# Attention maxima split into two parts behind their transposition, and two batches' gathers moved into a feed-forward part

## The reference, cut to what matters

```python
anchor_B = qk @ W_anchor.T * SCALE            # logits: 64 anchors for each row and head
attn = jax.nn.softmax(anchor_B, axis=-1)
s = jnp.sum(attn, axis=-2)
out = jnp.einsum('bhna,bhnd->bhad', attn, v)
out = recip[..., None] * out                  # recip: 1 / s
out = jnp.einsum('bhna,bhad->bhnd', attn, out)
...
h = jax.nn.silu(_tlin(x, w1_w, w1_s)) * _tlin(x, w2_w, w2_s)
h = jax.nn.gelu(_tlin(h, h1_w, h1_s), approximate=False)
h = jax.nn.gelu(_tlin(h, h2_w, h2_s), approximate=False)
return _tlin(h, w3_w, w3_s)
```

## Time and profile before

| | us |
|---|---|
| median of 3 runs (804.94 to 808.8) | 805.0 |
| profiled execution, its time | 807.5 |
| its span | 805.8 |
| PE busy in the span | 658.6 |
| DVE, ACT, POOL busy | 567.5, 401.3, 270.6 |

### The profile page before, as it was taken

One profiled execution on the slowest core, in us unless ns is written; L12 is line 12 of the kernel. 1 busy time (PEld: TensorE's weight loads), 2 busy tenths in 40 slices (PEclk: granted clock), 3 DMA queues, 4 the chain that ended last, 5 costly groups with the idle time before them and its releaser, 6 DMA issues.

```text
span 805.8 us, 9652 instructions
## 1 busy us (share of the span) xinstructions
PE 658.6 (82%) x2985; PEld 474.4 (59%) x2985; DVE 567.5 (70%) x1443; ACT 401.3 (50%) x699; POOL 270.6 (34%) x228
## 2 busy tenths in 40 slices
PE   5855444029999997788989999989899989899897
PEld 2755444028888886344557754567656468555575
DVE  5876386317898883799587678877686976784663
ACT  4552313317777773244257544367444385442573
POOL 6652717700000004779312067302177202242100
PEclk9985755559999997599899999999999999999999
DMA  6404248477889851000000010000000000000000
GB/s 204 131 31 152 77 166 303 167 262 256 269 261 330 285 179 59 26 13 27 14 0 1 1 46 21 13 2 1 29 24 27 0 1 1 26 1 1 0 1 27
DMA packets 26211, 69.26 MB, mean 86 GB/s; under 512 B 5344, under 2 KB 8432, under 8 KB 24688
## 3 DMA queue, kind: packets, MB, share of 16 engines
q1 hardware_dynamic: 22064, 60.24, 21.9%
q0 software_dynamic: 4096, 8.40, 3.4%
HBM read 46.46 MB, written 22.16 MB: 85 GB/s over the span
## 4 chain that ended last, share of the span: by engine, by line
PE 56%; DVE 18%; issue 7%; POOL 6%; ACT 5%; another core or an unknown queue 3%; DMA 3%; SPq 1%; DVEq 0%; ACTq 0%; POOLq 0%
PE ps L1702 14%; PE ps L1698 8%; PE ps L1704 8%; PE ps L1706 6%; PE ps L1705 6%; PE ps L1959 6%; POOL yb L653 2%; DVE stats L1065 2%; PE ps L1977 2%; PE ps L1947 2%; DVE ring L1584 2%; POOL misc L701 1%; DVE cmat L1658 1%; DVE yb L1484 1%
## 5 line engine op out<-in xcount | busy, mean ns | idle before, releaser
L653 POOL DMA_INDIRECT yb<-y_by_expert,ypos x64 | 64.8, 1013 | 166.6 <-DMA y_by_expert<-ysb 151.0
L1702 PE MATMUL ps<-hid,fh 128*128 128x512 f32 x256 | 103.6, 405 | 5.3 <-DVE hid L1568 5.3
L1704 PE MATMUL ps<-hid,fh 128*128 128x512 f32 x256 | 101.4, 396 | 0.0
L607 POOL DMA_INDIRECT rows_by_expert<-h,pos x64 | 64.7, 1011 | 53.4 <-DVE pos L1226 34.8
L701 POOL TENSOR_TENSOR misc<-misc,ring 128x1024 f32<-128x1024 f32 x28 | 66.1, 2360 | 32.6 <-DVE ring L1558 27.5
L1568 DVE TENSOR_TENSOR hid<-ring,hid 128x512 fp32r<-128x512 f32 x56 | 38.6, 689 | 42.0 <-ACT hid L944 40.1
L1959 PE MATMUL ps<-ring,hn 128*128 128x512 f32 x112 | 57.1, 634 | 9.2 <-DVE ring L1558 9.2
L1702 PEld LDWEIGHTS ps<-hid,fh 128*128 128x128 f32 x256 | 48.2, 188 | 21.3 <-DVE hid L1568 10.6
L1977 PE MATMUL ps<-attnT,cmat 128*128 128x512 f32 x128 | 56.9, 592 | 0.0
L1704 PEld LDWEIGHTS ps<-hid,fh 128*128 128x128 f32 x256 | 48.3, 189 | 10.7
L1002 ACT ACTIVATE ring<-ps 128x1024 f32<-128x1024 f32 x32 | 32.8, 1024 | 43.4 <-PE ps L1947 41.6
(11 more groups left out here) (324 smaller groups left out, 1702.9 us busy)
## 6 DMA issues: line engine op xcount, KB each, us to landing
wbuf<-w_split SPq DMA_DIRECT2D x46, 512.0 KB, 5.6
w_split<-parts SPq DMA_DIRECT2D x4, 2048.0 KB
raw<-in_w SPq DMA_DIRECT2D x8, 512.0 KB
xs<-rows_by_expert SPq DMA_DIRECT2D x16, 256.0 KB, 5.5
y_by_expert<-ysb SPq DMA_DIRECT2D x16, 256.0 KB, 4.7
rows_by_expert<-zeros SPq DMA_DIRECT2D x9, 256.0 KB, 2.2
xa<-in_x SPq DMA_DIRECT2D x4, 512.0 KB, 4.8
ffn_raw<-in_ffn SPq DMA_DIRECT2D x2, 1024.0 KB
```

The costliest lines, as they stand in the source:

```text
L607: gp.indirect_dma_start(disp, bass.IndirectOffsetOnAxis(pos[:, b, k, t:t + 1].bitcast(U32), 0), h1[:, b % 2, t, :], None).then_inc(scatter ...
L653: gp.indirect_dma_start(yb[:, k, t, :], None, ydisp, bass.IndirectOffsetOnAxis(ypos[:, b, k, t:t + 1].bitcast(U32), 0))\
L1702: te.matmul(out_, w(0), x(0), start=first, stop=False)
L1704: return te.matmul(out_, w(0), x(1), start=False, stop=last_)
```

## The change

Two things are changed. First, DVE no longer splits the maxima ahead of the transposition. The 128x16 maxima are transposed whole; ACT's copy to `mTs`, rows 0 to 15, is the rounded part, and DVE takes the remainder from PSUM, 16x128, into rows 32 to 47 of `mTs` (`max_remainder`, event `dve_mlo`). Rows 16 to 31 are zero, set once. `shift`, and the half-1 transposition that overwrites bank 1, wait for `dve_mlo` in the place of `act_maxT`. `max_remainder(t)` stands in DVE's queue behind `sums(t-1)`, and for tile 0 behind the second `neg_max` (batch 0) or the residual of the feed-forward part (the other batches). Second, POOL's gathers for batches 2 and 3 are taken out of the attentions of batches 1 and 2 and stand behind the modulation in the feed-forward part of batches 0 and 1. Those for batch 1 stay.

```diff
-        onehot = sb("onehot", [32, 1024], F32R)
+        onehot = sb("onehot", [48, 1024], F32R)
...
-        mTs = sb("mTs", [32, 128], F32R)
+        mTs = sb("mTs", [48, 128], F32R)
...
-        m32 = sb("m32", [128, 2, 2 * H], F32R)
...
+        dve_mlo = Events(sem("dve_mlo"), ts)
...
-                if more:
-                    gather(b + 1, places[0:2])
+                if b == 0:
+                    gather(1, places[0:2])
...
-                    if more and t < T - 2:
-                        gather(b + 1, places[2 * t:2 * t + 2])
-                if more:
-                    gather(b + 1, places[2 * (T - 2):])
+                    if b == 0 and t < T - 2:
+                        gather(1, places[2 * t:2 * t + 2])
+                if b == 0:
+                    gather(1, places[2 * (T - 2):])
...
                     for g in gs2:
                         modulate(g, b + 1)
+                if b + 2 < B:
+
+                    gather(b + 2, places)
...
-                copy(mTs[:, :], ps[0:32, 1, 0:128]).then_inc(*act_maxT.raise_(t))
+                copy(mTs[0:H, :], ps[0:H, 1, 0:128]).then_inc(*act_maxT.raise_(t))
...
+            v.tensor_copy(mTs[:, :], zeros[0:48, 0, :])
...
             def neg_max(t, b):
                 dve.wait_ge(*pe_logits.now(t, b))
-                k0, i = 2 + 2 * (t % 2), t % 2
-                if t >= 2:
-                    dve.wait_ge(*dve_max.now(t - 2, b))
-                settle(b, v.tensor_reduce(nmax[:, i, :], ps[:, k0:k0 + 2, :].rearrange("p k (h a) -> p (k h) a", a=A),
-                                          X, ALU.max, negate=True))
+                k0 = 2 + 2 * (t % 2)
                 if t >= 2:
                     dve.wait_ge(*pe_maxT.now(t - 2, b))
-                settle(b, v.tensor_copy(m32[:, i, 0:H], nmax[:, i, :]))
-                v.tensor_tensor(m32[:, i, H:2 * H], nmax[:, i, :], f(m32[:, i, 0:H]), ALU.subtract)\
-                    .then_inc(*dve_max.raise_(t))
+                v.tensor_reduce(nmax[:, t % 2, :], ps[:, k0:k0 + 2, :].rearrange("p k (h a) -> p (k h) a", a=A),
+                                X, ALU.max, negate=True).then_inc(*dve_max.raise_(t))
+
+            def max_remainder(t, b):
+
+                dve.wait_ge(*act_maxT.now(t, b))
+                v.tensor_tensor(mTs[32:32 + H, :], ps[0:H, 1, 0:128], f(mTs[0:H, :]), ALU.subtract)\
+                    .then_inc(*dve_mlo.raise_(t))
...
                     sums(t - 1, b)
+                    if t < T:
+                        max_remainder(t, b)
                     scaled(t - 1, b)
...
                 residual("F", 0, ffn_bank(0, "y"), b)
+                if more:
+                    max_remainder(0, b + 1)
...
-                transposes(1, [f(m32[:, t % 2, :])], 32).then_inc(*pe_maxT.raise_(t))
+                transposes(1, [nmax[:, t % 2, :]], H).then_inc(*pe_maxT.raise_(t))
 
             def shift(t, b):
-                pe.wait_ge(*act_maxT.now(t, b))
+                pe.wait_ge(*dve_mlo.now(t, b))
...
                     if h == 1 and t + 2 < T:
-                        pe.wait_ge(*act_maxT.now(t + 2, b))
+                        pe.wait_ge(*dve_mlo.now(t + 2, b))
```

More of the change, by code:

```diff
@@ L235, in build @@
         a_raw = at("a_raw", 0, [128, H * A])
-        oh_f = at("oh_f", 48, [32, 1024])
+        oh_f = at("oh_f", 48, [48, 1024])
         tri_f = at("tri_f", 52, [128, 128])
@@ L589, in _ @@
                              pattern=[[1, 128]], channel_multiplier=-1).then_inc(u_pool, 1)
-            for base in (0, -H):
+            for base in (0, -32):
                 v = oh_f[:, :].rearrange("p (h a) -> p h a", h=H)
@@ L1616, in _ @@
             neg_max(1, 0)
+            max_remainder(0, 0)
             hT_attn(1, 0)
@@ L1620, in _ @@
                 sums(0, b)
+                max_remainder(1, b)
                 if b == 0:
@@ L1628, in _ @@
                 sums(1, b)
+                max_remainder(2, b)
                 scaled(1, b)
@@ L1633, in _ @@
                 sums(2, b)
+                max_remainder(3, b)
                 scaled(2, b)
```

## The result

The changed kernel took 830.3 us (median; 829.5 to 838.0) where the kernel before took 805.0: a ratio of 1.0333, 95% interval 1.026 to 1.041. I had forecast 816.0, range 807 to 822. The sign is right, the size is not: plus 25 where I had plus 11. The execution that was profiled is one of 838.0 us, so its trace holds some 8 us that the median does not. Ratios and intervals are made of each kernel's fast runs alone (a run over 1.5% above its kernel's fastest counts as slow) and medians of all runs, so a ratio can differ from the quotient of the medians beside it.

The account below looks back on a forecast made before the run. The prediction took PE to bound batches 1 to 3, and POOL and DVE to hold batch 0. Terms 7.65 + 2.7 + 0.6 = 10.95, say 11.0, on 805.0 gave 816.0 us, range 807 to 822.

Parts of the forecast that it names:

- the gathers' new place: Sixteen gathers behind the modulation in each of two feed-forward parts, forecast to hold DVE's CASTs: 0.6 us in all.
- So it fits: Claim that the moved gathers, 20 us or somewhat more, end at 464 to 465, before the first product at 465.79.
- The wait of half 1: In attention tiles, half 1 of PE's transpositions waits for DVE's remainder; period 5.16 to 5.66, plus 0.50 us a tile.
- tiles 3 to 5: Tiles t = 3, 4, 5 of batches 1 to 3: 0.50 us each, 1.50 a batch.
- the next: Tile t = 6 of batches 1 to 3: 0.50 less 0.10 for the removed CAST, 0.40 us.
- the last: Tile t = 7 of batches 1 to 3: no logits follow, product already waiting for DVE's scaling, forecast 0.
- At the start: Start of attentions 1 to 3: 0.34 us for t = 2, and 0.31 for the first shift behind tile 0's remainder.
- Batch 0: Attention held by POOL and DVE: first shift 1.04 us late, remainders of tiles 2 and 3 later; 2.7 us in all.
- What was taken out: Gathers removed from the attentions of batches 1 and 2, forecast to give 0 in the tiles and behind them.
- the part on the maxima: The forecast's terms for the new wait: 7.65 us for batches 1 to 3 and 2.7 for batch 0.
- gathers too late: Rival: all sixteen gathers held, ending at 475, 9 us past the product behind them, in two batches; 834 us, chance 0.05.

## Why the prediction was wrong

**The step that failed** is the gathers' new place, which I had at 0.6 us (0.3 for each of two batches, with bounds of 0 and 1.0). "So it fits" was right: they end at 469.3, ahead of the product L686 at 479.9, and DVE's CASTs were hardly held (0.43 to 0.60 us beside them). But I had asked only what the gathers wait for and whom they hold by the shared memory, not what a row of sixteen does to the events of everybody else. In the first comparison the two stretches that hold them grew by 13.6 us together; beside the whole change without a stall (83.92 and 79.83) they are 9.1 and 5.6 us longer. Gathers alone, on a like chip, grew them by 4.7 and 4.8 against the other chip's 79.5 and 79.7. The case that this needs both edits was excluded. Eight gathers did nothing and pauses removed the stall, on a chip where sixteen in a row were not run, and traffic of the DMA engines does not do it on a chip without the stall. The warning stood in the trace of before, in sixteen scatters of layer 0 and the row of DVE behind "remote".

**The wait of half 1** was right in kind and nearly in size. On the clock of the tile the forecast and the trace agree step by step from the product on: sum at 1.19 (measured 1.16), reciprocal at 2.44 (2.42), remainder at 2.61 (2.70), its end at 2.90 (2.98), half 1 at 3.01 (3.10), and from there 2.65 us to the next product (2.65). The 0.09 is the hand-over from reciprocal to remainder, 0.28 between their starts where I took 0.17 from a range up to 0.25. The remainder takes 0.28 (I had 0.29 between 0.17 and 0.44). That it is a wait and not more work is shown by the run with the logits between the halves, which brings the period to 4.96, under that of before.

**By tile**, from the exponentials of batch 3 (intervals before: 3.49, 6.30, 5.15, 5.15, 5.15, 5.26, 3.94; after: 3.69, 6.43, 5.75, 5.75, 5.75, 5.75, 4.35): tiles 3 to 5 cost 0.60 each (I had 0.50), the next 0.49 (0.40), the last 0.41, which I had at 0 because its product waited for DVE's scaling anyway. That last one is the larger error: in DVE's queue the scaling stands behind the remainder too, which I read in the code only afterwards. At the start 0.33 over two intervals and 0.05 ahead of them, where I had 0.34 and 0.31. A batch costs 3.0 instead of 2.55, three batches 9.0 instead of 7.65.

**The clock at the start of attention 1** was not in the sum. PE's short waits there are followed in some runs by about 7 us at the lower clock, and the attention takes 39.4 instead of 37.45: 1.9 us more (in three of five runs with the new maxima and the old order, beside the first).

**Batch 0**, 2.7 in the forecast, is confirmed by rows only in its first step:

```profile
336.12 1.22 DVE L1541 TENSOR_REDUCE nmax<-ps 128x16 f32<-128x1024 f32 x1 [0.94 <-PE ps L1719]
336.23 0.27 ACT L730 ACTIVATE mTs<-ps 16x128 fp32r<-16x128 f32 x1 [6.21 <-PE ps L1711]
...
337.71 0.73 PE L1960 MATMUL ps<-onehot,mTs 48*128 48x512 f32 x2 [1.52 <-DVE mTs L1547]
```

The first shift starts 1.48 us behind the start of ACT's copy, where it was 0.32 before (332.56 and 332.88): 1.16 late, forecast 1.04. The whole of the batch can't be read off. Its stretches differ between runs with the same code there: attention 0 and what follows take 129.5 us in the trace of before, 125.8 with the gathers alone, 129.3 in the kernel before with the copies beside it, and 129.4 with the maxima alone. What is left of the maxima alone, 13.3 - 9.0 - 1.9 = 2.4 us of medians, is near it. Two small slips in the prediction's own numbers move no sum: 345.6 - 343.19 is 2.4 and not 2.45, and 4 x 0.8 is 3.2 and not 3.3.

**What was taken out** gave nothing, as forecast: attention 2 has 37.45 us with gathers in it (maxima alone) and without.

So the part on the maxima, 10.35 us by forecast, is 13.3 on the second chip and 12.8 by its ratio on 805 (11.4 to 14.2 by the interval). The gathers alone, by their ratio where they stall, are 7.2 of 805 (3.1 to 11.3), where I had 0.6. The two make 20 of the 25 us; with the 1.0223 of the maxima alone at 797 they make 25. The rest is within the intervals and was not assigned. Where nothing stalls, the whole change gives 1.0181 and 1.0195, which is 820 to 821 on 805 and inside the forecast's range. That would have been partly luck, since there the gathers cost nothing and the maxima 2 to 3 us more than forecast.

The chance of 0.05 for "gathers too late" at 834 was near the time for a wrong reason: nothing waited for the gathers.

## What stays open

What it is in such a chip that delays the events was not found. In six rows of gathers (two feed-forward parts of three traces) the first late event was one that PE raised 11 to 13 gathers into the row, and it was recorded 1.8 to 4.7 us late, at the 13th gather or behind it. The Trainium skill says in "DMA: Bandwidth & Descriptors", section "Why a DMA increments its semaphore by 16 and not by 1", that all 16 DMA engines add to the semaphore for each such DMA. The traces at 774 us agree, with 16 recorded updates a gather (1024 for 64 in eight of the ten, 1021 and 1015 in the others); those at 797 to 807 have 8 to 12 a gather. That other engines' updates queue up with these would fit both the late events and the missing records, but no run here shows it, and it would have to differ between chips.

The profile records these updates, and whether the recording has a part in the stall, no run tells either. That instructions are fetched late does not fit the rows: the waiting engine starts 0.02 to 0.03 us behind the record of its event, and POOL goes on. The two runs with traffic were not made on a chip of the other kind, and neither was a row of sixteen gathers on the one where eight, and fours with pauses, gave no stall.

## What to carry to other kernels

Before a burst of one kind is moved, look for a burst of that kind anywhere in the trace of before and read who waits behind it, above all behind a releaser that the profile can't name. A split that moves half of a hand-over to a second engine puts the wait behind that engine's whole queue; where PE is the bound, look for work of its own that can stand ahead of the wait, since 1.4 us of logits between the halves paid back 0.6 us a tile and more. Look first at who else is near the bound: with the old maxima the same order cost 0.2 us a tile, for want of time on DVE. A change that touches rows of DMAs should be timed more than once, on different chips and each time beside the kernel before: the same code gave 0.9986 and 1.0089.

## What the runs showed of the hardware

- Where the kernel before takes 774 us, no event in any of the ten traces came late. Where it takes 797 to 807, work that waited for PE's events started 4 to 7 us late in the feed-forward part and 8 us late in layer 0 (65.62 in the trace of before, for transpositions that ended at 57.53) near the end of a row of sixteen indirect DMAs. In the feed-forward part it was in time with eight, or with a pause after each four. Ahead of attention 0 in the trace of before, where eight gathers follow each other from 311.21 on, one copy of ACT (321.15) starts 1.9 us late.
- A subtraction of 16x128 with one operand in PSUM takes 0.28 us on DVE and starts 0.28 behind the start of the reciprocal ahead of it.
- An idle stretch of PE of 4 to 5 us is followed by about 7 us at 1.2 GHz (468.6 to 475.4 in the first stall). A gather product that falls into such a stretch takes 3.78 instead of 1.98 us (457.80 in the run with pauses).
- A CAST of 128x16 takes 0.17 us on DVE alone and up to 1.29 us beside POOL's addition of 128x1024.
